# A later switch to the full ring of slot tiles, another mix of scatters and moves, and one Newton pass for two norm groups

## The reference

```python
x = x + attention(layernorm(x))          # only positions 0..15 change beyond the bias ob
t = layernorm(x)
scores = sigmoid(t @ router.T)
topk = best 4 of 32 experts, out of the best 2 of 4 groups, by scores + bias
w = 2.5 * scores[topk] / sum(scores[topk])
mixed = sum_k w[k] * down[e_k] @ (silu(gate[e_k] @ t) * (up[e_k] @ t))
x = x + mixed + shared_expert(t)
```

## Time and profile before

| what | us |
|---|---|
| median of 3 runs (lowest, highest) | 442.76 (441.08, 446.77) |
| the profiled execution: its time, the span of its instructions | 442.9, 441.1 |
| PE busy | 363.4 (82%) |
| DVE busy | 303.3 (69%) |
| POOL busy | 301.9 (68%) |
| ACT busy | 238.5 (54%) |

### The profile page before, as it was taken

One profiled execution on the slowest core, in us unless ns is written; L12 is line 12 of the kernel. 1 busy time (PEld: TensorE's weight loads), 2 busy tenths in 40 slices (PEclk: granted clock), 3 DMA queues, 4 the chain that ended last, 5 costly groups with the idle time before them and its releaser, 6 DMA issues.

```text
span 441.1 us, 9457 instructions
## 1 busy us (share of the span) xinstructions
PE 363.4 (82%) x2368; PEld 295.4 (67%) x2368; DVE 303.3 (69%) x1097; ACT 238.5 (54%) x612; POOL 301.9 (68%) x438
## 2 busy tenths in 40 slices
PE   0468899999788898799959999999999999999200
PEld 0354666757346455588849899999989989998200
DVE  3669995963997965367524468885477847887847
ACT  1454693578564656557725566556555656655100
POOL 5511888677887887877878777777777776666300
PEclk9999996999999999999989999999999999999855
DMA  7990233432228968778965885652798898997796
GB/s 168 250 332 24 90 115 115 155 119 92 111 103 330 397 243 273 266 234 274 291 200 170 274 241 152 186 173 97 255 308 282 293 328 278 340 292 250 264 309 214
DMA packets 47033, 98.01 MB, mean 222 GB/s; under 512 B 8697, under 2 KB 30846, under 8 KB 45696
## 3 DMA queue, kind: packets, MB, share of 16 engines
q1 hardware_dynamic: 33968, 62.70, 45.9%
q0 software_dynamic: 12720, 34.62, 21.1%
q10 hardware_dynamic: 288, 0.03, 0.1%
HBM read 53.93 MB, written 44.57 MB: 223 GB/s over the span
## 4 chain that ended last, share of the span: by engine, by line
PE 63%; DVE 15%; DMA 9%; issue 4%; ACT 3%; POOL 3%; SPq 1%; POOLq 0%; DVEq 0%; ACTq 0%
PE two_banks L1192 24%; PE two_banks L1205 12%; PE two_banks L1016 7%; PE two_banks L1179 6%; PE two_banks L1067 5%; DMA loopb<-slots_dram 3%; PE two_banks L971 3%; DVE x_sb L1816 3%; DMA slots_dram<-loopb,slot_i 2%; PE two_banks L965 2%; DMA gu_w<-pairs_dram 1%; DMA pairs_dram<-routing,loopb 1%; POOL pairs_dram L766 1%; PE two_banks L1151 1%; DVE loopb L1599 1%
## 5 line engine op out<-in xcount | busy, mean ns | idle before, releaser
L756 POOL DMA_INDIRECT slots_dram<-loopb,slot_i x128 | 129.0, 1008 | 49.3 <-issue 25.4
L1192 PE MATMUL two_banks<-routing,staged_w 128*128 128x128 f32 x1096 | 145.8, 276 | 0.1
L1192 PEld LDWEIGHTS two_banks<-routing,staged_w 128*128 128x128 f32 x1096 | 134.1, 193 | 0.4 <-ACT routing L908 0.4
L1205 PE MATMUL two_banks<-dn_w,routing 128*128 x274 | 83.3, 386 | 1.5 <-DVE routing L1802 1.3
L1802 DVE TENSOR_TENSOR routing<-routing,two_banks 128x128 f32<-128x128 f32 x137 | 39.1, 286 | 65.6 <-ACT routing L913 59.2
L1842 DVE COPY staged_w<-gu_w 128x512 f32 x137 | 62.2, 455 | 15.7 <-issue 12.4
L913 ACT ACTIVATE routing<-two_banks 128x128 f32<-128x128 f32 x137 | 38.0, 277 | 57.6 <-PE two_banks L1192 57.5
L1016 PE MATMUL two_banks<-gu_w,sgu_w 128*128 128x512 f32 (+1 forms) x128 | 63.1, 624 | 3.1 <-DVE loopb L1599 2.3
L1179 PE MATMUL two_banks<-ident,loopb 128*128 128x128 f32 x274 | 52.9, 275 | 10.3 <-DMA loopb<-slots_dram 8.9
L908 ACT ACTIVATE routing<-two_banks 128x256 f32<-128x256 f32 x137 | 52.0, 380 | 13.3 <-PE two_banks L1179 13.3
L766 POOL DMA_INDIRECT pairs_dram<-routing,loopb x44 | 45.7, 1038 | 17.4 <-issue 15.3
(11 more groups left out here) (302 smaller groups left out, 514.6 us busy)
## 6 DMA issues: line engine op xcount, KB each, us to landing
loopb<-slots_dram SPq DMA_DIRECT2D x137, 128.5 KB, 2.8
routing<-pairs_dram SPq DMA_DIRECT2D x14, 512.0 KB, 5.3
loopb<-pairs_dram SPq DMA_DIRECT2D x10, 512.0 KB, 4.4
slots_dram<-blank SPq DMA_DIRECT2D x33, 136.0 KB, 27.1
gu_w<-in_gate_up SPq DMA_DIRECT2D x2, 2048.0 KB, 10.7
gu_w<-pairs_dram SPq DMA_DIRECT2D x8, 512.0 KB, 7.8
gu_w<-in_gate_up SPq DMA_DIRECT2D x6, 512.0 KB
x_sb<-in_x SPq DMA_DIRECT2D x2, 1024.0 KB, 13.9
```

The lines of the kernel that those rows point to most:

```text
L756: pool.indirect_dma_start(out=slots_dram, out_offset=bass.IndirectOffsetOnAxis(ap=slot_i[:, at:at + 1], axis=0), in_=xg[:, r, :] if n < TT ...
L1192: ins = pe.matmul(bank[2 + u % 2][:, m * P:(m + 1) * P], staged_w[:, u % 2, c, m * I:(m + 1) * I], xT[:, u % 2, c, :], start=(c == 0), sto ...
L1205: ins = pe.matmul(y_ps(u), hid[:, u % 2, 0:P], w, start=True, stop=True)
```

## The change

Four edits, none of which changes what is computed.

1. FIRST_LAPS is 32 instead of 24: tiles 24 to 31 use places 0 to 7 a fourth time, tile 40 is the first in place 8.
2. SOON: 2, 5 and 8 result scatters stand ahead of moves 29, 30 and 31, instead of 4, 9 and 14. All scatters and moves stay in POOL's list.
3. N2 is gone. N5 now makes the factors of groups 3 and 4 together and raises `norm_ready` by 2. N3 and N4 (bias and moments of group 4) and U1 stand ahead of the copy of the first attention step, N5 behind it.
4. In ACT's list the table loads Z0 and Z1 are gone, and S5 (stage of move 5) stands behind L20 instead of ahead of it.

```diff
-FIRST_LAPS = RING + RING // 2
+FIRST_LAPS = 2 * RING
...
-SOON = {TT - 3: 4, TT - 2: 9, TT - 1: 14}
+SOON = {TT - 3: 2, TT - 2: 5, TT - 1: 8}
...
# FILL_ACT, step 5, two pieces of the line
-    T17 L16 T18 L17 Z0 C1 G2 L18 D0 T19 S4 T20 T21 T22 L19 D1 S5 L20 Z1 L21 L22
+    T17 L16 T18 L17 C1 G2 L18 D0 T19 S4 T20 T21 T22 L19 D1 L20 S5 L21 L22
...
 FILL_DVE = [
-    "R0 R0 N6 R0 R0 R0 R0 P0 P1 P2 R0 R0 N0 U0 N1 N2 U1",
-    "N3 N4 N5 R1 R1 R1",
+    "R0 R0 N6 R0 R0 R0 R0 P0 P1 P2 R0 R0 N0 U0 N1 U1 N3 N4",
+    "N5 R1 R1 R1",
...
-                a, b = GROUPS_OF_TILES[3 + k // 3 % 2]
+                a, b = GROUPS_OF_TILES[3][0], TT
...
-                                             rstd[:, a:b], ALU.mult, ALU.mult).then_inc(norm_ready, 1)
+                                             rstd[:, a:b], ALU.mult, ALU.mult).then_inc(norm_ready, 2)
```

## The result

| what | before | changed |
|---|---|---|
| median (lowest, highest), us | 443.0 (441.08, 446.77) | 452.09 (449.32, 453.35) |
| ratio of the times, 95% interval | | 1.0186 (1.0104 to 1.0268) |
| the profiled execution: time, span, us | 442.9, 441.1 | 452.2, 450.4 |

Both medians are of 4 runs. The changed kernel is slower by 8.2 us (0.0186 x 443), with an interval of 4.6 to 11.9 us, and by 9.3 us between the two profiled spans. The forecast was 448.4 us. The range given was 440 to 453 us, and the forecast alone had 445.8 to 451.

A forecast was written before the change was run, and what follows sets the result against it. PE was taken as the busiest engine, with POOL's list saying when it may go on in the loop. 442.9 + 5.2 (head) + 0.3 (clock at tiles 79 to 85) + 0 (tiles 24 and 32) = 448.4 us, range 440 to 453.

The forecast's parts named there:

- The place of the gain: Loop, tiles 24 and 32: stalls go, PE gets tile 32 at 236.0 instead of 243.76, 7.75 us gained there.
- waits at tiles 79 and 80: Loop: PE, arriving early, has new waits of 3 to 4 us there, for load 79 and behind row fetches.
- the 5.2 of the sum: Head: 5.2 + 0.6 + 0.65 - 1.2 = 5.2 us later, bounds 2.9 and 7.4.
- The factors of group 3: Head, DVE: the merged pass for 15 tiles takes 2.68 us, group 3 is ready at 57.8, 7.1 us later.
- The clock behind the new wait: Head, PE: half speed after idling from about 53 to 58.4 costs 0.6 us, bounds 0 and 1.5.
- S5: Head, ACT: its new place ahead of L21 delays the logits and the next attention step, +0.65 us.
- The old slow stretch at 68 to 74 us: Head, PE: half speed there cost 3.0 us; three fifths of it were expected to recur, so -1.2 us.
- Nothing later takes this back: After the head: the 5.2 us shift stays through 70 to 175 us and moves POOL's list, scatter 63 and tile 85.
- rival (d): Clock: 3.0 us after the head's wait, old stretch recurs, 1.5 at tile 79's waits; 453.3 us, chance 0.13.
- (a): Loop: the 7.75 us gain stays, with the head's 5.2 us loss; 440.4 us, chance 0.14.
- (c): Loop's gain stays and the head's wait for T16 is absorbed; 435.2 us, chance 0.03.
- (b): Head: the wait for T16 is absorbed, loop's gain still given back; 443.2 us, chance 0.12.

The follow-up runs named there:

- e1_loop: The kernel before with the change's FIRST_LAPS and SOON alone, head as before: 442.42 us, 0.9993 of the kernel before.
- e2_head: The kernel before with the head's edits alone (one Newton pass for both groups, lists of DVE and ACT): 451.35 us, 1.0211 of the kernel before.
- e3_act: The kernel before with only ACT's list of the change (no Z0 and Z1, S5 behind L20): 443.62 us, 0.9995 of the kernel before.
- e14_ids_alone: The kernel before with row numbers kept apart, scatter waits written out and first row fetches later, without the loop edits: 442.07 us, 1.0006 of the kernel before.
- e5: The loop edits alone plus row numbers of all 137 tiles kept apart, so loads wait for no result scatter: 438.61 us, 0.9897 of the kernel before.
- e11_ids_waits: The loop edits with row numbers kept apart, plus the implied scatter waits written out ahead of row fetches: 439.21 us, 0.9913 of the kernel before.
- e12_late_rows: As e11_ids_waits, with the first row fetches moved behind loads 86 and 88 instead of 79 and 84: 438.53 us, 0.99 of the kernel before.
- the dose runs: The kernel before with DVE's list reordered, two passes, group 3 planned about 2.1 or 4.1 us later: 442.87 us (1.0021) and 447.97 us (1.0123).
- e13_fill_wait: The changed kernel with G2 and U2 of the shared expert ahead of T16 in PE's list: 450.99 us, 1.0222 of the kernel before.

## Why the prediction was right, and where it was off

**The loop: right.** The place of the gain (tiles 24 and 32, 7.75 us said, 7.3 measured in e1_loop), its end (zero at tile 85, 0.8 us measured; of both, 0.9 us come from the earlier head of that execution) and its cause (scatter 63 does not move) all held. Named signs: no wait of over 1 us at tiles 24 and 32 (none and 0.87), SP's longest wait 23 us (23.4), waits at tiles 79 and 80 (1.63 and 3.14, where I had said 3 to 4 for both). What I had not seen is the second limit, ACT's result copy that waits 2.69 us for an output buffer ahead of tile 75; it took part of the delay that I gave to tile 79. From tile 80 on PE was at half speed: tiles 80 to 82 took 5.93 instead of 3.09 us. Of these 2.84 us I had charged 0.3. They were hidden, since tile 85 still had to wait for its load. Against e2_head (336.42), with the old loop, tile 85 is 1.3 us later, but so is scatter 63 (317.23 against 315.94), and the medians are 0.7 us apart. In e1_loop tile 85 did not wait for its load: there PE itself was as late, 9.17 us from tile 80 to 85 (316.81 to 325.98) instead of 7.7, by the half clock. One reading was wrong without consequence: the prediction lets scatters 8 to 13 start 3.6 us later at most, but scatter 8 went out at 232.47 in e1_loop against 222.08 before, 10.4 us later. No tile there waited for its buffer.

**The head: right in mechanism, its size too small.** Step by step up to L1114, where 87.80 stands against 81.29 of before, 6.5 us instead of the 5.2 of the sum:

- The factors of group 3: 57.8 said, 58.46 measured. Most of the difference is ACT's silu, which DVE's U1 waits for and which was 0.5 us later in this execution; the pass itself took 2.80 for 15 tiles instead of 2.68, so its cost hardly grows with the tiles, as taken. T16 on PE: 5.2 us late said, 5.96 measured.
- The clock behind the new wait: 0.6 said, 1.64 measured (T16 to T18 in 4.55 instead of 2.91 us), above the upper bound of 1.5. I took the pieces behind T16 for short ones; G2 stands among them and ran in 3.01 instead of 1.88 us. This is the term that failed, by its size.
- S5: 0.65 said, 0.47 measured between T20 and T22, and nothing by L1114 (e3_act). It should have been zero.
- The old slow stretch at 68 to 74 us: -1.2 said, -1.6 measured, as a shorter one stood in its place (0.50 in 78 to 80 us). But that stretch is not a fixed part of the program. In e14_ids_alone, whose head is that of before, it is missing, as this window shows:

```profile
70.00:72.00 2.00, 1.76 (x4) 0.87 (x5) 0.18 (x1) 1.72 (x4) 1.76 (x3) 1.00 0.40 143
```

The step L1114 of before, and then of e14_ids_alone (there L1112):

```profile
81.29 0.42 PE L1114 MATMUL two_banks<-ident,routing 128*128 128x128 f32 x2
```

```profile
78.67 0.41 PE L1112 MATMUL two_banks<-ident,routing 128*128 128x128 f32 x2
```

Six profiled executions have the same instructions there (before, e1, e5, e11, e12, e14), with this step at 78.67 to 81.29: that of before was the latest. Measured against the 78.67 to 78.79 of the three that had no such stretch (e1, e5, e14), the changed head costs 9 us at this place, not 6.5. I built a credit into the sum from something that one execution happened to show; that this term came out near its value is luck.

"Nothing later takes this back" held, but the loss also grew, for which the sum had no term: move 16 is 6.75 us late, scatter 63 10 us. Of the 3.2 us in between 1.7 are clock again: at 134.39 eight products took 5.37 us, and the same eight 3.67 in the profile of before. It shows with the old head in other executions too (e1_loop was at 0.50 in 126 to 128 us). The rest arises from the start of the loop on. PE was at 0.50 in 190 to 192 us there, and tiles 1 to 3 took 5.08 instead of 3.59 us; in other executions, with the old head, they did too (5.16 in e1_loop, 5.08 in e11_ids_waits).

So the result, 452.1, lies nearer to rival (d), 453.3, than to the forecast, and it is partly luck that the range held. Two of (d)'s three causes are seen: a half clock of more than 0.6 us behind the new wait, and another in place of the old stretch; its 3.0 us for the first were too much. The third, the 1.5 us at tile 79's waits, did not show in the end. Rivals (a) and (c) fall with e1_loop, (b) with e2_head.

On the clock, the Trainium skill ("TensorE: Matmul & The Clock Gate", Part 1) puts the ramp at under 1% of a typical span. Here the three stretches that rows price cost 1.64, 1.70 (5.37 - 3.67) and 2.84 us (5.93 - 3.09), together 6.2 of 450.4 us, 1.4%. The last was hidden; without it the share is 0.7%, which is under the Trainium skill's figure. But the half clock is paid behind several waits here, and each of these terms is as large as those that the sum was made of.

## What to carry to other kernels

Saving operations on an engine is worth nothing if the first consumer of the result gets it later: merging two passes saved 2.7 us of VectorE's list (2.80 us instead of 2.86 and 2.68) and made the factors of the first of the two groups 7.7 us late, and the dose runs show that the cost starts where the next engine runs out of other work. Before a stall's removal is counted as a gain, follow the slowest queue behind it to its next waits and move the gain past each one; here it took further edits to keep 4 us, and a third wait took the rest. A half-speed stretch seen in one profile is not part of the program until a second execution shows it at the same place.

## What the runs showed of the hardware that was not expected

PE's clock fell to half behind a stretch in which it was partly busy as well: in e13_fill_wait the wait was 2.35 us and three shorter ones followed (0.56, 0.57 and 1.29 us), and the attention products ran at 0.50.

```profile
58.00:60.00 2.00, 0.81 (x4) 0.40 (x4) 0.00 (x0) 1.94 (x4) 1.80 (x4) 1.00 0.34 119
60.00:62.00 2.00, 0.45 (x3) 0.20 (x2) 0.00 (x0) 1.90 (x3) 1.64 (x3) 0.80 0.35 133
...
64.00:66.00 2.00, 2.00 (x11) 2.00 (x11) 1.76 (x12) 2.00 (x5) 1.07 (x2) 0.50 0.37 139
```

In 136 to 138 us of the changed kernel PE was at 0.50 while busy throughout. Where such stretches fall differs between executions of the same instructions, and moves the step at L1114 by up to 2.6 us. And a load of 128.5 KB (3.0 us from issue to landing in the median of the changed kernel) took 9.84 us in e12_late_rows when it was issued behind two fetches of 0.5 MB and a store of 1 MB. That the order of issue on SP's queue is part of its price is a guess; no run changed that order alone.
